# ScalarE weighs each gathered result in place, VectorE sums a token tile's six at once, and x comes back to where the gathered rows stood

## The reference, cut to what matters

```python
xn = _layernorm(x)                                    # x: 2 x 1024 tokens x 256 features
s  = attn(xn)                                         # matmul, rope, tanh, group norm, transpose
g  = silu(shared_ffn(xn) + moe(xn))                   # two shared and 32 routed experts
x  = x + s * g

def moe(xf):                                          # six of 32 experts per token
    idx, w = _route(xf, Wr, br)
    gate = zeros((T, E)).at[arange(T)[:, None], idx].add(w)
    for w1, w2, g in zip(W1, W2, gate.T):             # written as a scan
        acc += g[:, None] * (square(relu(xf @ w1.T)) @ w2.T)
```

## Time and profile before

| | |
|---|---|
| median of 3 runs | 397.77 us |
| the profiled execution's own time | 400.36 us |
| its span | 398.6 us |
| mean granted TensorE clock | 0.936 |
| busy: PE, DVE, ACT, POOL | 78%, 67%, 60%, 56% of the span |

### The profile page before, as it was taken

One profiled execution on the slowest core, in us unless ns is written; L12 is line 12 of the kernel. 1 busy time (PEld: TensorE's weight loads), 2 busy tenths in 40 slices (PEclk: granted clock), 3 DMA queues, 4 the chain that ended last, 5 costly groups with the idle time before them and its releaser, 6 DMA issues.

```text
span 398.6 us, 8202 instructions
## 1 busy us (share of the span) xinstructions
PE 309.3 (78%) x2716; PEld 235.5 (59%) x2716; DVE 266.6 (67%) x631; ACT 241.0 (60%) x383; POOL 221.6 (56%) x235
## 2 busy tenths in 40 slices
PE   0566885999979888778888787899955976998750
PEld 0344643676758677667667666775731664886530
DVE  4688889898942656566757564557631866788666
ACT  4788799445667657667666685984720744444322
POOL 2966879847776354646636465202674674666410
PEclk9996898799998989999899899999995998999996
DMA  8941150554852463646637455525543474666731
GB/s 273 371 161 53 56 191 2 157 157 152 278 153 81 135 189 108 217 128 190 208 107 213 134 174 170 153 75 192 167 134 103 146 224 118 193 189 190 196 109 67
DMA packets 40490, 62.90 MB, mean 158 GB/s; under 512 B 5218, under 2 KB 28930, under 8 KB 40450
## 3 DMA queue, kind: packets, MB, share of 16 engines
q1 hardware_dynamic: 33202, 42.57, 33.2%
q0 software_dynamic: 7248, 19.80, 17.3%
HBM read 46.66 MB, written 15.70 MB: 156 GB/s over the span
## 4 chain that ended last, share of the span: by engine, by line
PE 44%; DVE 18%; issue 11%; ACT 8%; DVEq 7%; another core or an unknown queue 4%; DMA 3%; POOL 2%; ACTq 1%; SPq 0%
DVE xs L1281 5%; PE rot L908 5%; DVEq L1283 4%; PE hp L931 3%; PE hp L946 3%; PE hp L945 3%; PE hp L944 3%; DVE hf L1257 3%; PE hp L933 3%; PE dp L1000 2%; PE bp L891 2%; PE dp L1002 2%; PE dp L1003 2%; PE hp L932 2%
## 5 line engine op out<-in xcount | busy, mean ns | idle before, releaser
L605 POOL DMA_INDIRECT xgt<-xtab,ids x91 | 92.8, 1019 | 69.8 <-PE rot L908 40.9
L687 ACT ACTIVATE hf<-hf 128x512 f32<-128x512 f32 (+2 forms) x80 | 50.0, 625 | 83.9 <-DVE hf L1257 64.2
L616 POOL DMA_INDIRECT wst<-ytab,slot x60 | 61.4, 1024 | 37.5 <-DVE xs L1281 25.1
L1000 PE MATMUL dp<-wt,hhi 128*128 128x256 f16 x204 | 56.3, 276 | 8.4 <-DVE hlo L1264 5.0
L1274 DVE COPY wst<-rot 128x512 f32<-128x512 f32 (+1 forms) x35 | 23.8, 681 | 52.2 <-PE rot L961 43.2
L1257 DVE SCALAR_TENSOR_TENSOR hf<-hp,gate_bc 128x512 f32<-128x512 f32 x48 | 33.0, 687 | 37.1 <-PE hp L946 15.1
L1003 PE MATMUL dp<-wt,hhi 128*128 128x256 f16 x204 | 56.1, 275 | 1.4 <-issue 1.3
L1002 PE MATMUL dp<-wt,hlo 128*128 128x256 f16 x204 | 56.3, 276 | 0.9 <-issue 0.9
L944 PE MATMUL hp<-xh,wt 128*128 128x512 f16 (+1 forms) x148 | 51.2, 346 | 6.6 <-DVE hf L1257 3.9
L692 ACT ACTIVATE hhi<-hf 128x512 f16<-128x512 f32 (+2 forms) x80 | 50.0, 625 | 5.7
L945 PE MATMUL hp<-xh,wt 128*128 128x512 f16 (+1 forms) x148 | 51.3, 347 | 2.0 <-issue 1.9
(11 more groups left out here) (174 smaller groups left out, 712.5 us busy)
## 6 DMA issues: line engine op xcount, KB each, us to landing
gate_bc<-gtab SPq DMA_DIRECT2D x48, 256.0 KB
ytab<-wst SPq DMA_DIRECT2D x45, 256.0 KB
wst<-in_wts SPq DMA_DIRECT2D x17, 512.0 KB, 5.7
xs<-in_x SPq DMA_DIRECT2D x4, 512.0 KB, 5.5
xn<-in_x SPq DMA_DIRECT2D x16, 128.0 KB
out<-xn SPq DMA_DIRECT2D x16, 128.0 KB
xtab<-xn SPq DMA_DIRECT2D x3, 512.0 KB, 3.1
xgt<-xtab,ids POOLq DMA_INDIRECT x91
```

The source lines that it names most:

```text
L605: nc.gpsimd.indirect_dma_start(xg[:, a % XRING, :, :].rearrange("p h d -> p (h d)"), None, xtab, bass.IndirectOffsetOnAxis(ids[:, a:a + 1] ...
L616: nc.gpsimd.indirect_dma_start(yk[:, n % KRING, :], None, ytab, bass.IndirectOffsetOnAxis(slot[:, n // K, n % K:n % K + 1], 0))\
L687: nc.scalar.activation(hf[:, k % HP, 0:width(k)], hf[:, k % HP, 0:width(k)], ACT.Square, scale=W_SCALE ** (-0.5 if gated else -1.0))
L1000: nc.tensor.matmul(o, hhi[:, k % HRING, hcols], hi, start=(e == 0 and q % 2 == 0), stop=False, skip_group_check=True)
```

## The change

ScalarE gets a new step. After the high half of unit k it multiplies each result of that step, in its buffer of the ring, by the token's weight (`weigh_result`), in the order and at the steps in which VectorE added them before. VectorE no longer adds result by result. One step after a tile's sixth result is weighed it reduces the six buffers into `hbs` (a tile that nobody needs by then) and adds that to the accumulator: two instructions per tile, and the tile's six buffers come free together. Each routed tile is finished one step later in the plan. The rows of x come back by four loads of 512 KB, one per chunk of four tiles, into the space where the gathered token rows and their transposes stood (`xb` over `xgt`), at steps 51 to 54, after the first matmuls of the unit behind the last slots. SP no longer waits for a store before it goes on.

```diff
@@ -206,6 +206,8 @@
         hots = xgt[:, 0:2 * OHRING * P * K].rearrange("p (w s r k) -> p w s r k", w=2, k=K, r=P)
         wq_sb = xgt[:, 2 * OHRING * P * K:2 * OHRING * P * K + 2 * KC * D].bitcast(F32).rearrange("p (k d) -> p k d", d=D)
         spare = xgt[:, 2 * OHRING * P * K + 2 * KC * D:2 * OHRING * P * K + 2 * KC * D + 2 * P].bitcast(F32)
+
+        xb = xgt[:, :].bitcast(F32).rearrange("p (j d) -> p j d", d=D)
         one_a = hots[:, 0]
         one_b = hots[:, 1]
         hf = sb("hf", [P, HP, CH])
@@ -350,7 +354,7 @@
 
             pair = j // (2 * J) * J + j % J
             if j in ROUTED:
-                whole = ADD_AT + K * (ROUTED.index(j) + 1) // 2
+                whole = ADD_AT + K * (ROUTED.index(j) + 1) // 2 + 1
             else:
                 whole = last_of[j // J] + 4
             return max(whole, SM_AT(pair) + 1)
@@ -361,9 +365,12 @@
         finishing = lambda k: [j for j in FINISH if finish_at[j] == k]
         END = after + 2
 
+        AGAIN = sorted(range(NCH), key=lambda c: min(finish_at[j] for j in range(c * J, (c + 1) * J)))
+
         block = ctx.enter_context(nc.Block())
         pairs_at = lambda k, at: [p for p in range(PAIRS) if at(p) == k]
         by_quad = lambda a: a[:, :, :, :].rearrange("p h k (c r jj) -> p h k c r jj", c=NCH, jj=J)
+        x_chunk = lambda a, c: a[c * J:(c + 1) * J].rearrange("n p d -> (n p) d").rearrange("(r jj) d -> r jj d", jj=J)
         x_tile = lambda a, j: a.rearrange("n p d -> (n p) d").rearrange("(c r jj) d -> c jj r d", c=NCH, jj=J)[j // J, j % J]
 
         by_act = lambda k: k < EARLY or UNITS[k][0] == "slots"
@@ -465,14 +472,13 @@
                     sp.dma_start(ytab[own[0] * P:(own[-1] + 1) * P, :].rearrange("(a p) d -> p a d", p=P),
                                  ysb[:, v % YRING, 0:len(own), :]).then_inc(y_stored[v % YRING], 16)
 
-            def load_again(f):
-                if f >= J:
-                    sp.wait_ge(out_stored[f % J], 16 * (f // J))
-                sp.dma_start(xn[:, f % J, :], x_tile(x, FINISH[f])).then_inc(x_again[f % J], 16)
+            def load_again(c):
+                sp.wait_ge(l1_done, LAST + 1)
+                sp.dma_start(xb[:, c * J:(c + 1) * J, :], x_chunk(x, c)).then_inc(x_again[c], 16)
 
             def store_out(f):
                 sp.wait_ge(rows_ready, f + 1)
-                sp.dma_start(x_tile(out, FINISH[f]), xn[:, f % J, :]).then_inc(out_stored[f % J], 16)
+                sp.dma_start(x_tile(out, FINISH[f]), xb[:, FINISH[f], :]).then_inc(out_stored[f % J], 16)
 
 
             W_LOADS = {EARLY: 10, EARLY + 1: 11, EARLY + 2: 12, EARLY + 3: 13, PLACED: 14, PLACED + 1: 15, PLACED + 2: 16}
@@ -510,16 +516,13 @@
                 if k == PLACED:
                     store_gates(1)
                     sp.wait_ge(gt_stored, 16 * len(BLOCKS))
-                if k == EARLY + 2 * LEAD:
-                    for again in range(J):
-                        load_again(again)
                 if k - 2 in leaves and UNITS[k - 2][0] == "slots":
                     store_y(k - 2)
                 for j in finishing(k - 2):
                     store_out(f)
-                    if f + J < NT:
-                        load_again(f + J)
                     f += 1
+                if 3 <= k - LAST < 3 + NCH:
+                    load_again(AGAIN[k - LAST - 3])
             assert f == NT
             for s in range(J):
                 sp.wait_ge(out_stored[s], 16 * (NT // J))
@@ -720,6 +723,12 @@
                     act.wait_ge(sum_done, BLOCKS.index(c) + 1)
                     nc.scalar.activation(acc[:, own[0]:own[-1] + 1, :], dp[:, h, 0:len(own), :], ACT.Copy,
                                          scale=1.0 / W_SCALE).then_inc(sum_out, 1)
+
+            def weigh_result(n):
+                act.wait_ge(yk_landed[n % KRING], 16 * (n // KRING + 1))
+                act.wait_ge(wk_ready, n // K + 1)
+                nc.scalar.activation(yk[:, n % KRING, :], yk[:, n % KRING, :], ACT.Copy, scale=wk[:, n // K, n % K:n % K + 1])\
+                  .then_inc(yk_weighed, 1)
 
             def silu_sum(j):
                 f = FINISH.index(j)
@@ -811,6 +820,8 @@
                 for c in BLOCKS:
                     if k == last_of[c] + 3:
                         leave_sum(c)
+                for n in range(adds_by(k - 1), adds_by(k)):
+                    weigh_result(n)
                 for j in finishing(k):
                     silu_sum(j)
 
@@ -1244,7 +1255,7 @@
                 dve.drain()
                 nc.vector.tensor_tensor(e, e, gate[:, j:j + n, :].unsqueeze(2).broadcast_to([P, n, K, E]), ALU.mult)
                 dve.drain()
-                nc.vector.tensor_reduce(wk[:, i:i + n, :], e, AX.X, ALU.add)
+                nc.vector.tensor_reduce(wk[:, i:i + n, :], e, AX.X, ALU.add).then_inc(wk_ready, n)
 
             def relu(k):
                 dve.wait_ge(l1_done, k + 1)
@@ -1273,13 +1284,15 @@
                     dve.wait_ge(wlo_pool, POOL_STEPS)
                 nc.vector.tensor_copy(ysb[:, v % YRING, 0:len(own), :], rot[:, bank_of["leave", k, h], 0:len(own), :]).then_inc(y_out, 1)
 
-            def add(n):
-                j = ROUTED[n // K]
-                dve.wait_ge(yk_landed[n % KRING], 16 * (n // KRING + 1))
-                if n == 0:
+            def add(i):
+
+                j, at = ROUTED[i], i * K % KRING
+                dve.wait_ge(yk_weighed, K * (i + 1))
+                if i == 0:
                     dve.wait_ge(shared_out, len(shared_no))
-                nc.vector.scalar_tensor_tensor(acc[:, j, :], yk[:, n % KRING, :], wk[:, n // K, n % K:n % K + 1],
-                                               acc[:, j, :], ALU.mult, ALU.add).then_inc(yk_used, 1)
+                nc.vector.tensor_reduce(hbs[:, :], yk[:, at:at + K, :].rearrange("p k d -> p d k"), AX.X, ALU.add)
+                dve.drain()
+                nc.vector.tensor_tensor(acc[:, j, :], hbs[:, :], acc[:, j, :], ALU.add).then_inc(yk_used, K)
                 dve.drain()
 
             def finish(j):
@@ -1288,8 +1301,8 @@
                 dve.wait_ge(sm_ready, j // (2 * J) * J + j % J + 1)
                 nc.vector.tensor_tensor(acc[:, j, :], tz[:, f % 2, :], sm[:, j, :], ALU.mult)
                 dve.drain()
-                dve.wait_ge(x_again[f % J], 16 * (f // J + 1))
-                nc.vector.tensor_tensor(xn[:, f % J, :], acc[:, j, :], xn[:, f % J, :], ALU.add).then_inc(rows_ready, 1)
+                dve.wait_ge(x_again[j // J], 16)
+                nc.vector.tensor_tensor(xb[:, j, :], acc[:, j, :], xb[:, j, :], ALU.add).then_inc(rows_ready, 1)
 
             def one_hot(i):
 
@@ -1405,8 +1418,8 @@
                     group_var(p)
                 for p in pairs_at(k, NORM_AT):
                     group_norm(p)
-                for n in range(adds_by(k - 1), adds_by(k)):
-                    add(n)
+                for i in range(adds_by(k - 2) // K, adds_by(k - 1) // K):
+                    add(i)
                 for j in finishing(k - 1):
                     finish(j)
 
```

More of the change, by code:

```diff
@@ L237, in build @@
         yk_landed = [sem(f"yk_landed{s}") for s in range(KRING)]
-        x_again = [sem(f"x_again{s}") for s in range(J)]
+        x_again = [sem(f"x_again{c}") for c in range(NCH)]
         out_stored = [sem(f"out_stored{s}") for s in range(J)]
@@ L295, in build @@
         sm_ready = sem("sm_ready")
+        wk_ready = sem("wk_ready")
+        yk_weighed = sem("yk_weighed")
         yk_used = sem("yk_used")
```

## The result

The changed kernel takes **395.99 us** (median of 17 runs, 392.76 to 400.38) beside 398.07 us of the kernel before (17 runs): ratio 0.9937, 95% interval 0.9911 to 0.9963. That is 0.6% faster, clear of noise but within the 1% that the prediction counted as no change; 387.5 us was predicted. The profiled execution took 394.92 us, span 393.1.

A forecast was written before the change was run, and what follows sets the result against it. After about 280 us it saw PE stalls during gather runs, then DVE pacing steps 65 to 79 with late gates. 400.4 - 3 - 4.5 - 8.5 + 4.1 = 388.5, 385.9 against the median; it said 387.5 us, range 379 to 399.

The forecast's parts named there:

- C: Steps 65 to 79: 40.5 us for 49.0, so -8.5 (ends -11.6 and -3), PE and DVE about equal.
- The extrapolation: DVE's new reduction of 1536 numbers, priced from the 512-number reductions at 0.98 ns per further number: 1.68 us, taken as 1.7.
- a rival of 0.18: Gathers or reduction set the pace, by long landings or a strided reduction at 3.3 us: 398 us against the median; chance 0.18.
- over 2.5 us the forecast would be wrong: Sign against the forecast, in DVE's new reduction: it takes over 2.5 us instead of 1.7.
- B: Steps 57 to 65: 22.5 us for 27.0, so -4.5 (ends -5.6 and 0), as the 4.98 us wait should not return whole.
- A: Stall before relu 57: shorter gather run gains about 6 us, loads of x cost 3, so -3 (ends -8 and +6).
- ACT's new work is hidden by DVE and PE: Steps 65 to 79: two weighing passes per step, 0.8 us, bring ACT to 2.3 of at least 2.67 us, so hidden.
- a case of A = +3: Before relu 57: if PE's gaps are not instruction fetch, this stretch costs +3 and the result is 6 us later.
- D: Tail from relu 78: 21.4 us for 17.3, so +4.1 (ends +2.5 and +6), the last six gathers waiting for the eighth tile's addition.
- The rival that they stop the gates (0.12): Relu 55 to 58: gate loads queue behind the four loads of x, giving 408 us on the median; chance 0.12.

The follow-up runs named there:

- again2: The changed kernel unaltered, run on a fast chip beside the kernel before: 361.12 us, ratio 1.0093.
- flat2: Repeat on a fast chip of the changed kernel with its reduction reading neighbouring numbers (wrong sums, timing only): 352.7 us, 0.9819 of the kernel before.
- flat: The changed kernel with its reduction reading six numbers side by side (wrong sums, same work), fast chip: 354.64 us, 0.9821 of the kernel before.
- x_only3: The kernel before with only the loads of x changed, third run, on a slow chip: 393.43 us, 0.987 of the kernel before.
- few_gathers: The changed kernel with only the first 12 of 60 gathers, fast chip: 360.11 us, 1.0035 of the kernel before.
- x_only: The kernel before with only the loads of x changed, its 60 additions kept, fast chip: 351.95 us, 0.9747 of the kernel before.
- tree: The changed kernel with the reduction replaced by one addition of three buffers to three, then three short additions: 354.75 us, 0.9826 of the kernel before.
- x_only2: Repeat on a fast chip of the kernel before with only the loads of x changed: 351.92 us, 0.9799 of the kernel before.

## Why the prediction was wrong

**C is the failed step** ("the reductions shown take 512 numbers in 679 ns [...] if it halved the rate, it would be 3.3 us [...] I take 1.7"). The extrapolation itself was good: side by side, 1536 numbers take 1.75 us. But this reduction reads with a stride of 256 numbers, and takes 2.83. I had that end, put it only into a rival of 0.18, and even wrote that over 2.5 us the forecast would be wrong. The 10.0 us between the 40.5 predicted for C and 50.5 measured divide so: the stride 3.3 (again2 against flat2); 1.4 that flat2 still lies over 40.5; 5.3 by which C is longer on the slow chip (50.5 against 45.2), where relus 66 and 69 wait 6.2 us for late signals of PE. The sum had no term for such waits in C; I had looked for what is left of them in B. (This sets a slow chip against a fast one and holds as far as the stride costs the same on both, which no run shows.) The rival named the right mechanism (reduction or gathers set the pace) with C = -3, B = -2.5 and 398 us, nearer to the result than the forecast; its other half, late landings, did not occur (0.6 us of waits of ACT's weighings for a landing, in the group of L730 above).

The stride is worth 8.4 us of the whole on a fast chip. Taken off 395.99, that would be 387.6, the forecast to 0.1 us; this is an estimate, as `flat` was not run on a slow chip, and the match would be luck: A was 5.6 us better than I said, and the late signals in C cost about as much.

**B** is 3.6 us over its 22.5. On one fast chip the summing part costs 4.6 here (27.0 for 22.4), 2.9 of it by the stride. The rest I did not try by itself; DVE's timeline of again2 shows the finish of the first routed tile held up behind ACT, whose square had waited 2.29 us for the relu behind the reduction:

```profile
276.08 0.69 DVE L1275 SCALAR_TENSOR_TENSOR hlo<-hf,hhi 128x512 f16<-128x512 f32 x1
279.52 0.42 DVE L1302 TENSOR_TENSOR xs<-tz,xn 128x256 f32<-128x256 f32 x1 [2.74 <-ACT tz L741]
```

ACT in that wait does group norm, two weighings (0.90) and loads a table (1.28) before the silu. I had said ACT's new work is hidden by DVE and PE; in sum it is, but not where one silu waits in line behind it.

**A** named the right cause, the run of gathers, with a size too small. I took 6 us for the shorter run and charged 3 for the loads of x. The run is worth 8.3 (29.1 in x_only3 against 20.8; 8.5 by pacing on one chip), and the loads cost nothing (29.1 in x_only3 against 29.4). I took the waits for pauses of PE, though; they are late signals, and with the shorter run relus 56 and 57 still wait 5.94 and 3.10 us. The Trainium skill (Runtime: NRT & Kernel Launch, Instruction fetch mechanics) says that instruction fetch by DMA is mostly hidden. From that I had made a case of A = +3; A was -8.6 on the slow chip and -1.5 on fast chips. Yet the trace agrees with the page as far as it goes: in the kernel before the instruction queues move no packet from 292.1 to 322.4 us, and the pauses of the earlier trace rows lie in that stretch. So they don't look like fetch, and my reading of them as fetch that is not hidden is not borne out.

**D** is 3.0 us over. Two reductions stand in it, at 2.83 + 0.43 and gaps 3.5 each where I took 2.25: 2.5 of it; again2 has 23.0 from relu 78. The gathers of the last tile, which I made its main term, are the smaller one: without them the tail is 1.1 shorter (few_gathers 17.1 from relu 79, again2 18.2).

**The loads of x** did what was said: x_only gives 0.9747 and 0.9799 on fast chips, 0.987 on a slow one. The rival that they stop the gates (0.12) did not occur: no relu waits for a gate, and relu 56 waits 5.94 us, before 6.42, at 262 GB/s and a DMA share of 0.78 over steps 51 to 57.

So the gain went like this on a slow chip, against x_only3 stage by stage: the summing part gives 8.3 us in A and 0.7 in B, and loses 6.2 in C and 4.9 in the tail, together -2.1 of the 5.2 that the loads of x bring by the same stages. And the 8.3 is a side effect, which one wait on POOL gives too.

## What to carry to other kernels

- Before a reduction replaces additions, price it with its own stride: fewer instructions are no gain where the one pass reads each number at a distance. A first pass over contiguous halves (`tree`) costs what the unstrided reduction does.
- An edit that only changes when buffers come free can be worth more than its arithmetic. Try the pacing first; it is one line. Here it gave 8.5 us on a slow chip, beside the loads of x, and nothing on fast chips.
- If two parts of a change have gains of opposite sign, only the parts apart show it: on fast chips 0.975 and 1.019 apart, 1.009 together. The product would be 0.993, so the parts do not simply multiply; they ran on different fast chips, and why they don't stays open.
- When an engine waits for another, look up when the work that it waits for ended. The pause that stands beside the wait in the trace can be a different one.

## What the runs showed of the hardware

- A reduction over six fp32 numbers 1 KB apart (128 x 1536 in, 256 out) takes 2.83 us, 1.75 with the numbers side by side.
- The same kernel takes 398 us on some chips and 359 on others; granted clocks (0.936 and 0.964 in the mean, 3% apart) don't explain it alone. The transposes of the gathered rows tell the two apart, first the kernel before on a slow chip:

```profile
L908 PE MATMUL rot<-id,xgt 128*128 128x128 f16 x364 | 30.0, 228 | 11.9 <-issue 11.1 <-DVE wst L1274 0.8
```

and then on a fast one, with no idle time of that kind:

```profile
L908 PE MATMUL rot<-id,xgt 128*128 128x128 f16 x364 | 27.4, 219 | 2.2 <-DVE wst L1274 2.2
```

These, too, are steps in which POOL gathers; 27 of the 39 us lie ahead of relu 51. What in the chips differs stays open. On a fast chip even 50 gathers in one run (x_only2) leave no such gap.
- On the slow chips PE's signals reach DVE up to 14.7 us after the matmuls' recorded end while POOL gathers in a run, on fast chips 0.04 to 0.5 us after it.
- ACT scales 128 x 256 fp32 numbers in place in 495 ns, two of them in 0.89 us.
